# A GpSimd write and a wait for it ahead of each of 880 gathers in a graph layer

## The chip, the cores and the metric

The kernel runs on one core of a Trainium2 chip. The metric is the device time of one execution in microseconds (us). The core's engines, by the names of the profile, are PE (TensorE's matmuls; PEld is its weight loads), DVE (VectorE), ACT (ScalarE), POOL (GpSimd) and SP (SyncE, which here only issues transfers). Each has its own queue of instructions and works through it in order; they meet through semaphores.

## The reference

The input is 3125 nodes of 256 features, 53125 edges with a source, a destination and one of 16 types, and the weights of three blocks. The part that matters here is the typed message pass, done once along the edges and once against them:

```python
def _typed_pass(feat, W, bias, src_idx, dst_idx, etypes, norm_per_edge, n):
    proj = jnp.einsum('ni,rio->rno', feat, W)
    m = proj[etypes, src_idx] + bias
    m = m * norm_per_edge[:, None]
    return segment_sum(m, dst_idx, num_segments=n)
...
x = x + gnn(layernorm(x)) + mixer(layernorm(x))
x = x + moe_ffn(layernorm(x))
```

`norm_per_edge` is one over the degree of the node that receives. The mixer is a linear attention and an MLP over the same nodes; the last block routes each node to 2 of 8 experts.

## The kernel before, in words

The program is written out instruction by instruction, one queue per engine, with every wait stated. Three parts of it concern the change.

**Projection.** For each direction PE multiplies 25 tiles of 128 nodes with 16 weight matrices: `project` (line 674), 200 slots per direction, two matmuls of 512 columns in each. ACT copies every result out (`evacuate`, line 667) and SP stores it to a table in device memory, `table_fwd` or `table_bwd` (`store_banks`, line 685): one row of 256 floats for each node and type.

**Gather and sum.** The edges are sorted on the chip into 440 groups of 128 per direction (`TE`), each group with receivers in one tile of 128 nodes. For group `n`, POOL issues an indirect DMA that fetches 128 rows of 1 KB from the table into one of 16 buffers (`RING = 16`, `gather`, line 721). PE multiplies the buffer with a one-hot matrix (`sum_tile`, line 738), and DVE adds the result into the accumulator of its node tile (`add_sums`, line 764). The semaphore `s_sm` counts finished sums; gather `n` waits until sum `n - 16` is done, so that its buffer is free. That is the wait on line 724, which goes through the helper `Engine.wait` (line 74; it leaves out a wait for zero or less, so gathers 0 to 15 have none).

**Order of the work.** PE's order is fixed when the program is written. The sums of the forward groups stand between the backward projection's slots (`forward_upto`, line 781), 424 of them by the last slot; the other 16 and the 440 backward ones stand between the steps of the mixer: its rows and keys (`rows_upto`, `keys_upto`), attention (`attn_upto`) and MLP (`mlp_step`), whose last step comes with the last sum. POOL's queue in the meantime holds the gathers alone (lines 990 to 996). Ahead of the first gather it waits for the forward table to be stored, ahead of gather 440 for the backward table. After gather 879 POOL helps with additions (line 1001), and in the last block it issues 56 gathers of tokens (line 1009) and 56 indirect adds of rows to the output (line 1017, in `add_rows`), each of which waits first for its rows (`s_o7`, line 1013) and then for the indirect add before it (`s_sc`, line 1016, again through line 74).

ACT's `evacuate` has, at every even slot but the first few, two waits as well: first line 670 (that the store buffer is free), then line 671 (that the projection is done), and at every odd slot line 671 alone.

Of the kernel before, what the change touches and what calls it, by code (L numbers as in the profile page):

```python
# [101 lines left out]
def build(nc, a, out):  # L102
# [12 lines left out]
    with ctx:  # L115
        def sb(name, cols, dt=f32, rows=P):
            return ctx.enter_context(nc.sbuf_tensor(name, [rows, cols], dt))
# [5 lines left out]
        def sem(name, whole=False):  # L123

            nsem[0] += 1
            s_ = nc.alloc_semaphore(f"{name}_{nsem[0]}")
            if not whole:
                scope.append(s_)
            return s_

        def sems(name, n, whole=False):
            return [sem(f"{name}{i}", whole) for i in range(n)]
# [44 lines left out]
        kmax = sb("kmax", C)  # L177
        Pm = sb("Pm", 512)
        gmap_b = sb("gmap_bwd", TE, i32, 1)

        s_v, s_a = sem("dve", True), sem("act", True)
        V = Engine(None, nc.vector, s_v)
# [106 lines left out]
        RING = 16  # L289
# [424 lines left out]
        oh = [ar(R2 + RING * W + j * P, P) for j in range(RING)]  # L714
        acc = [ar(ACCF, NT * W), ar(R1, NT * W)]
        NARROW, SEG = (1, 6, 7), (2, 3, 6, 7)
        s_ga = sems("gather", RING)
        s_oh, s_sm, s_ac, s_ones, s_zf, s_zb = (sem(n) for n in
            ("onehots", "segment_mm", "accumulated", "ones_set", "zero_forward", "zero_backward"))

        def gather(e, n):

            d, b = n // TE, n % RING
            G.wait(s_sm, n - RING + 1)
            e.indirect_dma_start(msg[b][:, 0:C], None, table[d], bass.IndirectOffsetOnAxis(  # L725
                ap=idx[d][:, n % TE:n % TE + 1], axis=0)).then_inc(s_ga[b], 16)

# [251 lines left out]
        with nc.Block() as block:  # L979
            @block.gpsimd  # L980
            def _(e):
# [8 lines left out]
                for n in range(TE):  # L990
                    gather(e, n)
# [3 lines left out]
                for n in range(TE, 2 * TE):  # L995
                    gather(e, n)
# [1014 lines left out]
```

## Time and profile before

| | us |
|---|---|
| median of 3 runs | 2249.82 (2246.55 to 2253.24) |
| the profiled execution | 2245.63 |
| its span, first to last instruction | 2243.7 |
| PE busy | 2015.8 (90%) |
| POOL busy | 1027.6 (46%) |
| DVE busy | 1138.3 (51%) |
| ACT busy | 605.0 (27%) |
| DMA engines, mean share over the span, queue of the gathers (q0) | 23.1% |

The profile is of one execution. Busy time counts an engine's own instructions, not its sequencer's waits and branches. PE's granted clock is 0.960 of full speed over the span. In a timeline row stand the start, the duration, the engine, the line, what is written and read, and in brackets how long the engine had been idle and what ended that; "issue" stands for time in which it waited for nothing that the profile shows, "remote" for a releaser that the profile doesn't know.

### The profile page before, as it was taken

The page shows a single profiled execution, that of the slowest core. Times are in us where ns is not written, and L with a number is a line of the kernel's source. Part 1 is how long each engine was busy: PE and PEld are TensorE (multiplying, and loading weights), DVE is VectorE, ACT ScalarE, POOL GpSimd, SP SyncE. Part 2 cuts the span into 40 slices and gives each one's busy share as a digit, 9 for nine tenths or more (in the row PEclk, how much of TensorE's full clock was granted, in tenths as well). Part 3 has the DMA queues.
Part 4 walks back from the last instruction along what each step waited for, and adds up shares of the span by engine and source line. Part 5 has one row for each costly group of instructions (what it writes and reads, how often), then busy time and mean ns, then how long its engine had stood idle before and what let it go on. Part 6 is the DMA issues. An engine that isn't in the chain of part 4 may idle for free.

```text
span 2243.7 us, 26429 instructions
## 1 busy us (share of the span) xinstructions
PE 2015.8 (90%) x8235; PEld 1379.3 (61%) x8235; DVE 1138.3 (51%) x2452; ACT 605.0 (27%) x1262; POOL 1027.6 (46%) x1014
## 2 busy tenths in 40 slices
PE   7999999889999999898878788898989669999997
PEld 3456544355555555454545555677777668888897
DVE  4999950256666564433566656544455841111121
ACT  2333333211221221111422221222222552222242
POOL 0000000366666666666566666666665113333332
PEclk9999999999999999999899999999999579999999
DMA  7432335455555555556644444332334384444473
GB/s 276 158 136 95 134 155 229 159 158 177 179 178 179 178 168 182 178 181 165 184 144 138 146 138 122 90 90 87 87 90 80 128 288 112 125 116 120 128 194 67
DMA packets 136486, 333.20 MB, mean 149 GB/s; under 512 B 25344, under 2 KB 65952, under 8 KB 135072
## 3 DMA queue, kind: packets, MB, share of 16 engines
q1 hardware_dynamic: 80064, 199.64, 24.5%
q0 software_dynamic: 52992, 130.09, 23.1%
q10 hardware_dynamic: 3296, 1.80, 0.3%
q8 instruction: 71, 1.16, 0.2%
q14 instruction: 63, 0.52, 0.1%
HBM read 202.71 MB, written 128.71 MB: 148 GB/s over the span
## 4 chain that ended last, share of the span: by engine, by line
PE 80%; issue 6%; another core or an unknown queue 5%; DVE 4%; ACT 3%; DMA 2%; DVEq 0%; POOL 0%; SPq 0%; ACTq 0%; POOLq 0%
PE bank L679 29%; PE bank L748 15%; PE bank L1947 9%; PE bank L1958 8%; PE bank L1867 4%; PE bank L1876 4%; PE bank L586 3%; DVE arena L773 1%; PE bank L1777 1%; PE bank L1805 1%; DMA table_fwd<-arena 1%; PE bank L1765 1%; PE bank L1844 1%; PE bank L1916 1%
## 5 line engine op out<-in xcount | busy, mean ns | idle before, releaser
L679 PE MATMUL bank<-arena,work 128*128 128x512 f32 x1600 | 741.9, 600 | 14.2 <-ACT arena L672 9.0
L773 DVE TENSOR_TENSOR arena<-arena,bank 128x257 f32 x880 | 370.8, 421 | 529.7 <-PE bank L748 284.1
L748 PE MATMUL bank<-arena 128*128 128x257 f32 x1760 | 499.2, 396 | 71.1 <-DVE arena L773 37.6
L725 POOL DMA_INDIRECT arena<-table_bwd,arena x440 | 428.3, 974 | 237.4 <-issue 99.0
L725 POOL DMA_INDIRECT arena<-table_fwd,arena x440 | 437.2, 994 | 212.8 <-issue 99.8
L679 PEld LDWEIGHTS bank<-arena,work 128*128 128x128 f32 x1600 | 301.3, 192 | 296.5 <-issue 270.8
L672 ACT ACTIVATE arena<-bank 128x512 f32<-128x512 f32 x400 | 238.5, 598 | 777.4 <-PE bank L679 551.7
L748 PEld LDWEIGHTS bank<-arena 128*128 128x128 f32 x1760 | 327.7, 197 | 194.8 <-issue 153.7
L1017 POOL DMA_INDIRECT out<-xn,work x56 | 89.4, 1597 | 250.9 <-DVE xn L192 181.3
L1947 PE MATMUL bank<-xn,arena 128*128 128x256 f32 (+1 forms) x1120 | 203.0, 340 | 0.0
L734 DVE TENSOR_TENSOR arena<-cst,arena 128x512 f32<-128x512 f32 x220 | 151.2, 689 | 102.0 <-PE bank L679 102.0
L1958 PE MATMUL bank<-arena 128*128 x896 | 199.0, 379 | 0.0
L1691 ACT ACTIVATE arena<-bank,work 128x256 f32<-128x256 f32 (+1 forms) x280 | 120.6, 431 | 286.7 <-PE bank L1947 278.5
L1947 PEld LDWEIGHTS bank<-xn,arena 128*128 128x128 f32 x1120 | 178.9, 192 | 17.0
L1486 DVE TENSOR_TENSOR xn<-bank,work 128x256 f32<-128x256 f32 x56 | 23.8, 425 | 321.5 <-PE bank L1958 321.5
L1958 PEld LDWEIGHTS bank<-arena 128*128 128x128 f32 x896 | 169.2, 190 | 22.4
L984 POOL MEMSET arena<- 128x6425 f32 x1 | 5.5, 5453 | 313.5 <-DVE gmap_bwd L193 313.5
L1867 PE MATMUL bank<-arena 128*128 128x256 f32 (+1 forms) x416 | 111.2, 390 | 25.7 <-ACT arena L1642 14.8
L1876 PE MATMUL bank<-arena 128*128 128x256 f32 x400 | 106.4, 388 | 8.0 <-ACT arena L1642 6.2
L1867 PEld LDWEIGHTS bank<-arena 128*128 128x128 f32 x416 | 79.2, 198 | 45.7 <-ACT arena L1642 19.4
L586 PEld LDWEIGHTS bank<-arena,work 128*128 128x128 f16 x832 | 67.2, 97 | 51.1 <-issue 46.5
L508 DVE TENSOR_TENSOR arena<-arena 128x648 f16<-128x648 f16 (+1 forms) x156 | 92.4, 607 | 8.8 <-PE bank L586 7.1
(315 smaller groups left out, 1563.8 us busy)
## 6 DMA issues: line engine op xcount, KB each, us to landing
table_fwd<-arena SPq DMA_DIRECT2D x100, 512.0 KB
table_bwd<-arena SPq DMA_DIRECT2D x100, 512.0 KB
arena<-in_W SPq DMA_DIRECT2D x35, 1024.0 KB
arena<-in_W SPq DMA_DIRECT2D x2, 4096.0 KB, 14.3
arena<-table_fwd,arena POOLq DMA_INDIRECT x440
arena<-table_bwd,arena POOLq DMA_INDIRECT x440
work<-x_transposed SPq DMA_DIRECT2D x50, 128.0 KB
mix_rows<-arena SPq DMA_DIRECT2D x25, 256.0 KB
```

The lines of the kernel that those rows point to most:

```text
L586: last = pe.matmul(ps[bank][:, 0:2 * LT].rearrange("p (v l) -> p v l", v=2), ohv[:, c // QB, :, c % QB], abv[:, :, c // QB, :, c % QB], st ...
L672: act.activation(ar(STG0 + s % 8 * 512, 512), ps[4 + s % 2][:, :], ACT.Copy).then_inc(s_po, 1)
L679: last = pe.matmul(ps[4 + s % 2][:, :], xT[t % 2][:, k * P:(k + 1) * P], ar(W_off[d] + k * 4096 + c * 512, 512), start=(k == 0), stop=(k = ...
L725: e.indirect_dma_start(msg[b][:, 0:C], None, table[d], bass.IndirectOffsetOnAxis(ap=idx[d][:, n % TE:n % TE + 1], axis=0)).then_inc(s_ga[b ...
L734: vec.tensor_tensor(oh_all[:, b:b + 4, :], iota.unsqueeze(1).broadcast_to(four), loc[n // TE][:, c:c + 4].unsqueeze(2).broadcast_to(four), ...
L748: pe.matmul(ps[sum_bank(n)][:, 0:W], oh[b], msg[b], start=True, stop=True).then_inc(s_sm, 1)
L773: vec.tensor_tensor(to, to, ps[sum_bank(n)][:, 0:W], ALU.add).then_inc(s_ac, 1)
L1691: act.activation(hT7[u % 2][:, j * C:j * C + n], ps[1 + j % 4][:, 0:n], ACT.Gelu, bias=aux[u % AR][:, 4 + j:5 + j]).then_inc(s_c7, 1)
L1867: last = pe.matmul(ps[4 + j % 2][:, 0:n], ar(W1T_off + k * HID + j * P, P), z2T[:, k * C:k * C + n], start=(k == 0), stop=(k == 1))
L1876: pe.matmul(bank, hT[:, j * C + u * P:j * C + (u + 1) * P], ar(W2T_off + j * C, C), start=(j == 0), stop=False)
L1947: last = pe.matmul(ps[1 + j % 4][:, 0:n], w1b[u % 4][:, k * HID + j * P:k * HID + (j + 1) * P], xT7[u % 2][:, k * C:k * C + n], start=(k = ...
L1958: last = pe.matmul(ps[5 + t % 2][:, 0:C], h, arena[:, ds(x * 2048 + (WE2 + j * C), C)], start=(j == 0), stop=(j == 7))
```

## The change

`gather` first writes zeros to a new tile of one column, `pause`, with a memset on GpSimd that adds one to a new semaphore, `s_pause`. After the wait for a free buffer and ahead of the indirect DMA it waits until `s_pause` has reached `n + 1`, that is, until this memset is done. Nothing reads the tile.

```diff
         gmap_b = sb("gmap_bwd", TE, i32, 1)
+        pause = sb("pause", 1)
...
-        s_ga = sems("gather", RING)
+        s_ga, s_pause = sems("gather", RING), sem("pause")
...
         def gather(e, n):
 
             d, b = n // TE, n % RING
+            nc.gpsimd.memset(pause[:, :], 0.0).then_inc(s_pause, 1)
             G.wait(s_sm, n - RING + 1)
+            e.wait_ge(s_pause, n + 1)
             e.indirect_dma_start(msg[b][:, 0:C], None, table[d], bass.IndirectOffsetOnAxis(
                 ap=idx[d][:, n % TE:n % TE + 1], axis=0)).then_inc(s_ga[b], 16)
```

## Rows read from the trace of the kernel before

**Rows 1.** The page, the chain that ended last, by engine.
```profile
PE 80%; issue 6%; another core or an unknown queue 5%; DVE 4%; ACT 3%; DMA 2%; DVEq 0%; POOL 0%; SPq 0%; ACTq 0%; POOLq 0%
```

**Rows 2.** Groups of POOL: busy us, mean ns, idle before and what ended it.
```profile
L725 POOL DMA_INDIRECT arena<-table_fwd,arena x440 | 437.2, 994 | 212.8 <-issue 99.8 <-PE bank L748 65.2 <-remote 43.4
L725 POOL DMA_INDIRECT arena<-table_bwd,arena x440 | 428.3, 974 | 237.4 <-issue 99.0 <-PE bank L748 95.3 <-remote 34.9
```

**Rows 3.** The line of the gathers: durations in ns (least, median, most), who waited.
```profile
L725 POOL DMA_INDIRECT arena<-table_fwd,arena x440: 940/946/1496, 420.7 to 1065.4; - x147
L725 POOL DMA_INDIRECT arena<-table_bwd,arena x440: 940/946/1412, 1074.6 to 1731.1; - x147
...
who waited for it (us, times):
  PEld bank L748: 3.7, 1
  PE bank L748: 2.8, 1
```

**Rows 4.** Windows, instructions of line 748 alone: PE and PEld busy (count), clock, DMA.
```profile
420.00:800.00 380.00, 132.97 (x488) 86.79 (x488) 0.98 0.56 173
420.00:1066.00 646.00, 229.77 (x848) 153.65 (x848) 0.98 0.57 174
```

**Rows 5.** Windows, instructions of line 725 alone: POOL busy (count), clock, DMA.
```profile
420.00:800.00 380.00, 260.87 (x258) 0.98 0.56 173
420.00:1066.00 646.00, 436.90 (x440) 0.98 0.57 174
```

**Rows 6.** Windows, all: PE, PEld, DVE, ACT, POOL busy (count), clock, DMA.
```profile
420.00:1066.00 646.00, 588.52 (x2109) 342.64 (x2107) 341.61 (x758) 126.11 (x227) 436.90 (x440) 0.98 0.57 174
1075.00:1732.00 657.00, 553.76 (x2289) 418.72 (x2289) 374.37 (x913) 158.23 (x353) 427.90 (x440) 0.95 0.40 116
```

**Rows 7.** Timeline of POOL, the first gathers, and around the last forward one.
```profile
416.21 0.13 POOL L986 MEMSET arena<- 128x16 f32 x1 [96.78 <-PE bank L679]
420.70 1.14 POOL L725 DMA_INDIRECT arena<-table_fwd,arena  x1 [4.36 <-DMA table_fwd<-arena]
...
1060.40 0.94 POOL L725 DMA_INDIRECT arena<-table_fwd,arena  x1 [1.45 <-PE bank L748]
1061.65 0.95 POOL L725 DMA_INDIRECT arena<-table_fwd,arena  x1 [0.30 <-issue]
...
1074.61 0.94 POOL L725 DMA_INDIRECT arena<-table_bwd,arena  x1 [8.27 <-DMA table_bwd<-arena]
```

**Rows 8.** Timeline of PE: the first two sums, and the last two (two instructions each).
```profile
424.89 1.14 PE L748 MATMUL bank<-arena 128*128 128x257 f32 x4 [2.84 <-DMA arena<-table_fwd,arena]
...
1744.38 1.03 PE L748 MATMUL bank<-arena 128*128 128x257 f32 x4
```

**Rows 9.** Timeline of POOL, its memsets at the start, back to back.
```profile
0.25 0.10 POOL L2005 MEMSET const-float32-0.0<- 128x1 f32 x1 [0.25 <-issue]
0.28 0.10 POOL L2005 MEMSET const-float32-1.0<- 128x1 f32 x1
```

**Rows 10.** The chain that ended last, the kernel's end: start us, us, what.
```profile
2228.12 0.36 DVE xn L192
2228.49 0.39 issue
2228.88 3.62 DMA out<-xn,work
2232.49 0.02 issue
2232.52 0.02 POOLq L74
2232.54 0.77 issue
2233.31 1.55 POOL out L1017
```

**Rows 11.** Timeline of SP, the transfer that waits for the backward table as well.
```profile
1073.84 0.81 SPq L1083 DMA_DIRECT2D arena<-in_mW1T  x2
```

**Rows 12.** The chain that ended last, in the backward projection.
```profile
922.67 0.02 ACTq L671
922.68 0.04 issue
922.73 0.60 ACT arena L672
```

**Rows 13.** Waits of PE from 420 to 1745 us: total us, times, longest.
```profile
PE bank L748 <- DVE arena L773: 37.6, 24, 6.8
```

## The prediction

> **What bounds the kernel now.** I began with the chain of waits that ended last. PE holds 80% of it and POOL none to speak of [rows 1]: matmuls set the time, and a POOL instruction is free as long as the gathers keep ahead of the sums.
>
> How far ahead are they? The groups of POOL show 880 gathers with a mean of (437.2 + 428.3) / 880 = 0.98 us [rows 2]. By the row of their line, 440 start from 420.7 to 1065.4, so one per 644.7 / 439 = 1.469 us, and 440 from 1074.6 to 1731.1, one per 656.5 / 439 = 1.495 us [rows 3]. Is that POOL's own pace or one imposed on it? Two gathers that wait for nothing stand 1.25 us apart, 0.95 us of work and a gap of 0.30 us; now and then one waits, as at 1060.40, for a sum of PE [rows 7]. The windows say the same: by 800 us there are 258 gathers [rows 5] and 488 / 2 = 244 sums, by 1066 us 440 gathers and 848 / 2 = 424 sums [rows 4]. So POOL runs 14 to 16 groups ahead, which is the whole ring, and PE waited for a gather once or twice in 1312 us (3.7 and 2.8 us) [rows 3]. PE, busy for 588.5 of 646 and 553.8 of 657 us [rows 6], paces the gathers through `s_sm`.
>
> POOL's spare time is then small: 1.469 less its own pace. That pace is the mean duration, 0.98, and 0.30, so 1.28 us; the spare is 0.19 us a gather forward and 0.21 backward. What the change adds up to 0.19 us costs nothing (PE hides it). Beyond that POOL becomes the bound, 880 times over. The question is the length of the stop.
>
> **The stop, step by step.** (1) The memset stands in POOL's queue behind gather n-1, so it is done only after that one. From the gather's end to the memset's start no row shows this pair; the ends are 0.03 us (four memsets back to back start 0.03 us apart, [rows 9]) and 0.30 us (gather to gather, [rows 7]). I take 0.10: a memset is nearer to the first, and even alone a gather begins late (below). (2) The memset of one column: 0.10 us [rows 9], 0.13 us for 16 columns on the same partitions [rows 7]. I take 0.11. (3) From the semaphore to the gather's start. Here lies most of the cost, and it depends on which of the two waits rides with the gather.
>
> [...] In the chain at the kernel's end the indirect add of L1017 has two waits, first `s_o7`, then `s_sc` by the helper on L74, and a row of POOL's queue bears the name of the second: POOLq L74, 0.02 us [rows 10]. ACT's evacuation has first L670, then L671, and again the second stands alone, ACTq L671 [rows 12]. So the first wait in the order of the program rides. In the changed gather `s_sm` comes first, and the wait for `s_pause` stands alone ahead of the indirect DMA from gather 16 on.
>
> What does that cost? At the end the scatter lands at 2232.49, the lone wait ends at 2232.54, and the next indirect DMA starts 0.77 us later; from landing to start 0.82 us. When the last wait to be met is the one that rides, VectorE's result, which ends at 2228.48, releases the same instruction in 0.40 us at most [rows 10]. Gather 440 has lone waits too: the backward table's landing starts an SP transfer at 1073.84 [rows 11] and the gather at 1074.61 [rows 7], 0.77 us. [...] I take 0.76 us from the memset's end to the gather's start, by the gather's own row; the ends are 0.40 us (the preparation hidden after all) and 0.82 us.
>
> Period of a gather: 0.98 + 0.10 + 0.11 + 0.76 = 1.95 us, against 1.469 and 1.495 now. Ends: 0.98 + 0.03 + 0.10 + 0.40 = 1.51, and 0.98 + 0.30 + 0.13 + 0.82 = 2.23 us.
>
> [...]
>
> **The sum.** The first gather starts at 420.70 [rows 7]. Gathers 1 to 15 have only the new wait, which rides. The 0.40 us above hold VectorE's own way out as well, so I take 0.28: 0.98 + 0.10 + 0.11 + 0.28 = 1.47 us each, 22.1 us together, to 442.8. The other 864 take 1.95 us: 1684.8 us, to 2127.6. The last sum follows its gather's start by what the first ones show with an empty ring: 424.89 less 420.70 is 4.2, less for later ones; I take 3.2, to 2130.8. Today the last sum starts at about 1744.9 (the second of the pair from 1744.38 [rows 8]). The difference is 386 us. The pause of 8.27 us ahead of gather 440 [rows 7] goes: sum 424, with the last backward projections, then runs some 3 us behind gather 424, 15 gathers or 29 us ahead of gather 439, and the stores end in that time. The uniform 864 periods have this in them already.
>
> What is behind POOL's wait? Its queue holds only gathers until 879. PE's sums wait for them, and behind these, since PE's order is fixed, all the projections and the mixer. Does PE keep up? It needs (588.5 + 553.8) / 880 = 1.30 us a group [rows 6], DVE 0.81 us, and the ring still evens out stretches of PE without sums. So POOL's period sets the stretch. Outside it nothing moves: after the last sum the program is the same, 499 us. The 880 memsets themselves (97 us) are within the period.
>
> Against the profiled execution: 2245.6 + 386 = 2631.6 us. That execution lies 4 us under the median of the three runs, so a median might be 2636; I stay between them at 2632.
>
> **The rivals.** (a) No change. If the wait for `s_pause` rode with the gather (or the preparation overlapped the wait), the period would be 1.47 us, today's, and the ring's head start would even out the rest: 2246 to 2252 us. It decides at 0.19 us of added time a gather. For it: the added instruction alone is 0.11 us, and its write is trivial. Against it: both pairs of waits in the trace leave the second alone. [...] (c) Longer: the memset starts 0.30 us after the gather and the lone wait costs 0.82, period 2.23: 442.8 + 1926.7 + 3.2 - 1744.9 = +628 us, 2873 us. For it: the gap of 0.30 us is the only one that follows a gather in the trace. (d) Faster: the stop lets VectorE, which shares work on the same memory, run without POOL beside it. PE waited 37.6 us for VectorE's additions at the sums [rows 13], so 2208 us at best, and only with all of the stop hidden.
>
> **How the numbers follow.** The forecast, a period of 1.85 to 2.14 us: 0.80, and by the same sum 2545 to 2796 us. (a) 0.08, (b) 0.05, (c) 0.05, (d) 0.02. The range 2530 to 2800 holds the forecast and the upper end of (b), a little over 8 in 10. The runs of before spread by 0.3%, about what can be told from no change, 7 us. Faster by more: (d), 0.02. Within: (a), 0.08. Slower: the forecast, (b) and (c), 0.90.
>
> **What would show it.** In the changed trace: a POOLq row of the new wait, or POOL's gathers without idle time ended by `s_sm`; starts of gathers 1.95 us apart, 1.47 us for the first 15; a memset 0.1 us behind each gather's end, then some 0.76 us idle before the next; PE waiting for gathers at L748 hundreds of times where it was once; sums level with gathers in the windows, not 14 behind; last gather near 2127 us; PE's share of the chain far under 80%; no 8 us gap ahead of gather 440; and 499 us after the last sum as now. It would be wrong if the starts stay 1.47 us apart (the wait is hidden), if the memset starts or lasts much later or longer than 0.2 us in all, or if PE falls behind on its own at the lower granted clock that idle time may bring (0.95 to 0.98 now).

## The result, and the profile after

The changed kernel takes 2546.13 us (median of 4 runs, 2543.91 to 2552.76) against 2249.09 us for the kernel before on the same chip: a ratio of 1.1326, 95% interval 1.1306 to 1.1347. The profiled execution took 2552.76 us, its span is 2550.9 us. The forecast was 2632 us.

First the chain that ended last, by engine (the page of the changed kernel; before in [rows 1]):

```profile
PE 52%; DMA 31%; issue 8%; POOL 7%; ACT 2%; DVE 0%; POOLq 0%; DVEq 0%
```

PE has fallen from 80% to 52%, and what has come in is the landing of gathers (DMA) and POOL. The line of the gathers and who waited for it (durations in ns; before in [rows 3]):

```profile
L728 POOL DMA_INDIRECT arena<-table_fwd,arena x440: 944/944/1464, 419.1 to 1234.5; - x147
L728 POOL DMA_INDIRECT arena<-table_bwd,arena x440: 944/944/1422, 1236.3 to 2048.7; - x147
...
who waited for it (us, times):
  PEld bank L751: 573.2, 579
  PE bank L751: 326.9, 431
```

From start to start the gathers now need (1234.5 - 419.1) / 439 = 1.857 us forward and (2048.7 - 1236.3) / 439 = 1.851 us backward, against 1.469 and 1.495. PE's matmuls waited for them 431 times, where they had waited once.

The timeline of POOL shows the stop itself, first at gathers 14 to 16, then where the tables change (before in [rows 7]):

```profile
438.54 0.95 POOL L728 DMA_INDIRECT arena<-table_fwd,arena  x1 [0.27 <-POOL pause L725]
439.49 0.11 POOL L725 MEMSET pause<- 128x1 f32 x1
439.87 0.94 POOL L728 DMA_INDIRECT arena<-table_fwd,arena  x1 [0.27 <-POOL pause L725]
440.81 0.11 POOL L725 MEMSET pause<- 128x1 f32 x1
441.68 0.94 POOL L728 DMA_INDIRECT arena<-table_fwd,arena  x1 [0.75 <-issue]
...
1234.45 0.94 POOL L728 DMA_INDIRECT arena<-table_fwd,arena  x1 [0.75 <-PE bank L751]
1235.40 0.11 POOL L725 MEMSET pause<- 128x1 f32 x1
1236.26 0.94 POOL L728 DMA_INDIRECT arena<-table_bwd,arena  x1 [0.75 <-issue]
```

The reader is to see three things. Each memset starts with the end of the gather ahead of it (439.49, 440.81) and takes 0.11 us. Gathers 1 to 15, which have the new wait alone, start 0.27 us after the memset; from gather 16 on, with both waits, 0.75 us after it. And the pause of 8.27 us ahead of the first backward gather is gone. That the 0.75 us are behind a lone wait shows in the chain (start us, us, what):

```profile
1005.56 0.12 POOL pause L725
1005.68 0.02 issue
1005.71 0.02 POOLq L727
1005.72 0.70 issue
1006.42 0.94 POOL arena L728
```

POOLq L727 is the wait for `s_pause`, and 0.70 us of "issue" follow it, as 0.77 us followed the lone wait of [rows 10].

How far the gathers are ahead: in the windows from 420 to 1066 us, line 751 alone (PE, PEld), then line 728 alone (POOL); before in [rows 4, 5]:

```profile
420.00:1066.00 646.00, 217.13 (x694) 115.03 (x694) 0.97 0.46 141
```
```profile
420.00:1066.00 646.00, 344.21 (x349) 0.97 0.46 141
```

694 / 2 = 347 sums stand against 349 gathers: the ring is empty where it had been full. What is left after the last sum (from 2052 us; PE, PEld, DVE, ACT, POOL):

```profile
2052.00:2551.00 499.00, 450.88 (x2388) 405.70 (x2388) 137.13 (x350) 173.38 (x408) 156.26 (x128) 0.92 0.52 144
```

The last sum starts at 2052.28 us, 307.5 us later than before (1744.82), and the span has grown by 307.2 us. The whole loss lies in the stretch of the gathers.

### The profile page after: what moved, and what is told of

It reads as the page before. It is cut to its first block, busy times and chain, and to the rows that moved or that the text cites. A ratio compares the mean times of both kernels' runs of the same rounds, so it can differ in the third digit from the quotient of the medians.

```text
span 2550.9 us, 28172 instructions
## 1 busy us (share of the span) xinstructions
PE 2140.6 (84%) x8235; PEld 1358.7 (53%) x8235; DVE 1149.7 (45%) x2452; ACT 606.8 (24%) x1262; POOL 1117.9 (44%) x1894
## 4 chain that ended last, share of the span: by engine, by line
PE 52%; DMA 31%; issue 8%; POOL 7%; ACT 2%; DVE 0%; POOLq 0%; DVEq 0%
PE bank L680 18%; DMA arena<-table_bwd,arena 15%; DMA arena<-table_fwd,arena 14%; PE bank L751 11%; PE bank L1950 8%; PE bank L1961 7%; POOL arena L728 6%; PE bank L587 2%; PE bank L1879 1%; POOL pause L725 1%; DMA table_fwd<-arena 1%; PE bank L1919 1%; ACT arena L1677 1%; PE bank L1780 1%; PE bank L1939 1%
## 5 line engine op out<-in xcount | busy, mean ns | idle before, releaser
L751 PE MATMUL bank<-arena 128*128 128x257 f32 x1760 | 590.0, 428 | 339.9 <-DMA arena<-table_bwd,arena 171.8
L751 PEld LDWEIGHTS bank<-arena 128*128 128x128 f32 x1760 | 291.2, 196 | 626.5 <-DMA arena<-table_bwd,arena 309.9
L728 POOL DMA_INDIRECT arena<-table_bwd,arena x440 | 423.0, 961 | 341.1 <-PE bank L751 218.0
L1961 PEld LDWEIGHTS bank<-arena 128*128 128x128 f32 x896 | 169.2, 190 | 22.4
L1645 ACT ACTIVATE arena<-bank,small 128x256 f32<-128x256 f32 (+1 forms) x104 | 48.5, 466 | 237.7 <-PE bank L1870 213.1
L725 POOL MEMSET pause<- 128x1 f32 x880 | 99.3, 113 | 4.6 <-DMA table_fwd<-arena 3.8
```

What stands on the lines that cost most here:

```text
L725: nc.gpsimd.memset(pause[:, :], 0.0).then_inc(s_pause, 1)
L751: pe.matmul(ps[sum_bank(n)][:, 0:W], oh[b], msg[b], start=True, stop=True).then_inc(s_sm, 1)
L1961: last = pe.matmul(ps[5 + t % 2][:, 0:C], h, arena[:, ds(x * 2048 + (WE2 + j * C), C)], start=(j == 0), stop=(j == 7))
```

## The experiments

The diffs are against the changed kernel.

The preparation theory says: the 0.70 us between the row of the lone wait and its indirect DMA (the chain above) are exposed because the wait is met only after the gather ahead has ended; met earlier, they lie within that gather. No row of a trace shows what POOL does in these 0.70 us, or that anything is prepared; "preparation" is a name for the time that the runs below make appear and disappear. "Rides" is such a name too: it is said of the wait that has no row in POOL's queue, where the other, lone one has a row of 0.02 us (POOLq). The theory's rivals: the stop costs this however it is waited for, a further wait on the sequencer costs it whenever it is met, or the memset itself costs.

**A caution on the base.** The kernel before took 2249 us in the first session, 2079 in the second and 2231 in the third. What is called the second session here are two, on two different chips: 2078.61 us beside the first four experiments and 2079.94 beside the next four. The third ran on yet another chip. No program ran twice on one chip in different sessions, as far as the chips are known, so no run shows whether the chip makes the difference. Each experiment is compared with the kernel before in its own session.

**The waits in the other order.**

```diff
             nc.gpsimd.memset(pause[:, :], 0.0).then_inc(s_pause, 1)
-            G.wait(s_sm, n - RING + 1)
             e.wait_ge(s_pause, n + 1)
+            G.wait(s_sm, n - RING + 1)
```

> The changed kernel with its two waits in the other order: first for the memset, then for the free buffer, so that the wait for the memset rides with the gather and the one for the buffer stands alone. Preparation theory (the cost is the preparation of the indirect DMA, which the lone wait for the memset keeps from running beside the gather ahead): the first 15 gathers of the changed trace have a riding wait and start 0.27 us after the memset, so starts are 0.97 + 0.11 + 0.27 = 1.35 us apart where nothing else holds them, under the 1.469 that PE leaves; 2249 us, within 0.3%. Stop theory (a wait for a memset between two gathers costs 0.75 us however it is made): starts 1.81 us apart, 2546 us as changed.

Measured: 2155.68 us against 2078.61, ratio 1.0372 (1.0348 to 1.0397). Its timeline of POOL:

```profile
1002.01 0.11 POOL L725 MEMSET pause<- 128x1 f32 x1
1002.39 0.94 POOL L728 DMA_INDIRECT arena<-table_fwd,arena  x1 [0.27 <-POOL pause L725]
1003.33 0.11 POOL L725 MEMSET pause<- 128x1 f32 x1
1003.72 0.94 POOL L728 DMA_INDIRECT arena<-table_fwd,arena  x1 [0.27 <-PE bank L751]
```

Starts are 1.33 us apart (1.400 in the mean), near the 1.35 of the preparation theory, and 0.48 us of each stop are gone by the order of two lines. The stop theory falls. But the time did not return to that of the kernel before, as I had expected from the 1.469 us of the first session. In the second session PE leaves POOL less time, which the next runs show.

**The memset without a wait.**

```diff
-        pause = sb("pause", 1)
+        pause = sb("pause", 2 * TE, mybir.dt.uint8)
...
-            nc.gpsimd.memset(pause[:, :], 0.0).then_inc(s_pause, 1)
+            nc.gpsimd.memset(pause[:, n:n + 1], 0).then_inc(s_pause, 1)
             G.wait(s_sm, n - RING + 1)
-            e.wait_ge(s_pause, n + 1)
```

> The memset alone, of a column of its own for each gather (one byte wide, so that they fit), with nothing that waits for it. Preparation theory: 0.11 us more a gather at most, 1.28 + 0.11 = 1.39 us, hidden; 2249 us. A rival: the memset as an instruction on the same engine costs by itself, for example by a longer gap ahead of the gather that follows it (over 0.41 us from the gather's end to the next start, against 0.30 before): 2249 us plus 864 times what the period has over 1.48 us.

Measured: 2080.73 us, ratio 1.0002 (0.9992 to 1.0012).

```profile
1000.92 0.94 POOL L727 DMA_INDIRECT arena<-table_bwd,arena  x1 [0.19 <-PE bank L750]
1001.87 0.12 POOL L725 MEMSET pause<- 128x1 uint8 x1
1002.17 1.12 POOL L727 DMA_INDIRECT arena<-table_bwd,arena  x1 [0.19 <-issue]
```

Starts are 1.25 us apart, as without a memset: it lies inside the 0.30 us that POOL has between two gathers anyway. Even the 0.11 us that I had allowed are not paid. The memset as such costs nothing.

**The wait one gather ahead.**

```diff
-        pause = sb("pause", 1)
+        pause = sb("pause", 2)
...
-            nc.gpsimd.memset(pause[:, :], 0.0).then_inc(s_pause, 1)
+            nc.gpsimd.memset(pause[:, n % 2:n % 2 + 1], 0.0).then_inc(s_pause, 1)
             G.wait(s_sm, n - RING + 1)
-            e.wait_ge(s_pause, n + 1)
+            G.wait(s_pause, n)
```

> The memset as changed, but the gather waits for the memset ahead of the gather before it (s_pause has reached n, not n + 1; two columns in turn). The wait stands alone as in the changed kernel, but is met while gather n - 1 has only just begun. Preparation theory: the preparation runs beside gather n - 1 again; starts 1.25 to 1.42 us apart, 2249 us. Lone-wait theory (a further wait on the sequencer costs 0.7 us each time, whenever it is met): 1.81 us apart, 2546 us. In between, if the preparation outlasts what is left of gather n - 1: 0.7 us against 0.94 us, so it should not.

Measured: 2086.47 us, ratio 1.0038 (1.0027 to 1.0049).

```profile
1001.30 0.12 POOL L725 MEMSET pause<- 128x1 f32 x1
1001.61 0.95 POOL L728 DMA_INDIRECT arena<-table_bwd,arena  x1 [0.19 <-POOL pause L725]
1002.55 0.11 POOL L725 MEMSET pause<- 128x1 f32 x1
1002.86 0.95 POOL L728 DMA_INDIRECT arena<-table_bwd,arena  x1 [0.19 <-POOL pause L725]
```

The same memset and a lone wait in the same place, and the period is 1.25 us again instead of 1.81. Only the moment at which the wait is met has moved.

Its 8 us over the kernel before are clear of the interval, and the traces show where they lie. Eight gathers (113, 211, 309, 407, 505, 603, 701 and 799, that is every 98th) start 1.8 to 2.0 us after the end of the gather ahead, though their buffers had been free for 4 us or more. Beyond the usual 0.30 us these eight stops take 13 us; the second session's trace of the kernel before has none of them. Gather 113 (idle time behind its memset):

```profile
567.46 0.95 POOL L728 DMA_INDIRECT arena<-table_fwd,arena  x1 [1.69 <-issue]
```

Other gathers wait less for their buffers in turn, so that all gaps from gather 16 on are together 10 us longer than in the kernel before (288.4 against 278.4). What makes every 98th gather late is open: the stops stand at these gathers in the changed kernel too, in those with the waits swapped and in the one with a stop at every second gather. The two kernels of the same session without a memset or without a wait for it have none of this size there.

**A second wait that is always met.**

```diff
-            nc.gpsimd.memset(pause[:, :], 0.0).then_inc(s_pause, 1)
             G.wait(s_sm, n - RING + 1)
-            e.wait_ge(s_pause, n + 1)
+            e.wait_ge(s_pj, SLOTS)
```

> No memset. The gather of the kernel before, with a second wait behind the one for the free buffer, for the count of projections that was reached before the first gather. It stands alone on the sequencer and is always met. Preparation theory: nothing is exposed, starts 1.25 us apart where no sum is waited for, 2249 us. Lone-wait theory: 0.7 us more a gather, period 0.98 + 0.75 = 1.73 us at least, about 2475 us.

Measured: 2080.32 us, ratio 1.0001 (0.9991 to 1.0012). The line of the new wait, and POOL's timeline:

```profile
L726 POOLq EVENT_SEMAPHORE  x865: 17/17/43, 419.6 to 1559.8; - x173
```
```profile
1000.90 0.97 POOL L727 DMA_INDIRECT arena<-table_bwd,arena  x1 [0.30 <-issue]
1002.17 0.95 POOL L727 DMA_INDIRECT arena<-table_bwd,arena  x1 [0.30 <-issue]
```

865 lone waits are in the program and nothing is lost: the lone-wait theory falls. In these runs a lone wait costs only when it is met late: the gap between two gathers is 0.30 us here, as in the kernel before, and 0.11 + 0.75 us in the changed kernel.

No run was made for one rival: that POOL takes 0.7 us to go on from any lone wait that is met late, whatever stands behind it. The trace of the kernel before speaks against it. POOL's first addition (line 1001) has two waits, and the second, for ACT's result (`s_bw`, line 1000), stands alone and is met last:

```profile
1747.92 0.51 ACT L1657 ACTIVATE arena<-arena,small 128x256 f32<-128x256 f32 x1 [0.71 <-DVEq L1326]
1748.58 0.87 POOL L1001 TENSOR_TENSOR X<-X,arena 128x256 f32<-128x256 f32 x1 [16.53 <-ACT arena L1657]
```

ACT ends at 1748.43, the row of the lone wait starts at 1748.46, and the addition starts 0.10 us after that row, where an indirect DMA starts 0.70 to 0.77 us after it. ACT's copy likewise starts 0.04 us behind its lone wait [rows 12]. So the 0.70 to 0.77 us stand in these rows only ahead of an indirect DMA; for POOL this rests on one place in one trace.

**The kernel before and the changed one once more.** Nothing is edited.

> The kernel before, unchanged, for a trace beside the experiments: in their session it took 2079 us where it had taken 2249 us, and they show the same instructions outside the stretch of the gathers. Pace theory (in that session PE is quicker through the sums, so that POOL's own pace of 1.25 us and its longer gathers, 1.32 us in the mean, set the stretch): about 2079 us, starts 1.25 us apart and 1.32 in the mean, sums 3 to 18 us behind the gathers. If the session is like the first, 2249 us and 1.47 us.

> The changed kernel, unchanged. Preparation theory: POOL's period is its own and the same on any chip, 1.81 us and 1.86 in the mean, so the time is near 2546 us also where the kernel before takes 2079 us: the change then costs 864 x (1.862 - 1.318) = 470 us. Proportional rival (the session is quicker in all): 1.13 x 2079 = 2354 us.

Measured: 2079.38 us, ratio 1.0007 (0.9994 to 1.0019), and 2549.01 us, ratio 1.2254 (1.2227 to 1.2281). The line of the gathers in the kernel before, second session:

```profile
L725 POOL DMA_INDIRECT arena<-table_fwd,arena x440: 942/949/1458, 417.6 to 992.7; - x147
L725 POOL DMA_INDIRECT arena<-table_bwd,arena x440: 942/949/1465, 996.0 to 1569.0; - x147
...
who waited for it (us, times):
  PEld bank L748: 33.4, 41
  PE bank L748: 14.4, 26
```

Here 1.310 us (575.1 / 439 forward; 1.305 backward) separate two gathers, POOL's own 1.25 with its longer ones, and PE waits for some of them. In the second session POOL was already next to being the bound. The changed kernel has the period of the first session (1.863 against 1.862 us from gather 16 on) and its time: 2549 against 2546 us. So the time after the change is set by POOL's period, and what the change costs, 297 or 469 us, by what POOL had to spare. With 1.310 as the base the swapped kernel's +77 us are explained: 864 x (1.400 - 1.310) = 78.

**A stop at every second and at every fourth gather.**

```diff
-            nc.gpsimd.memset(pause[:, :], 0.0).then_inc(s_pause, 1)
+            if n % 2 == 0:
+                nc.gpsimd.memset(pause[:, :], 0.0).then_inc(s_pause, 1)
             G.wait(s_sm, n - RING + 1)
-            e.wait_ge(s_pause, n + 1)
+            if n % 2 == 0:
+                e.wait_ge(s_pause, n // 2 + 1)
```

The other has 4 in place of 2.

> The memset and the wait for it, with the free-buffer wait first as in the changed kernel, at every second gather alone. Preparation theory: starts alternately 1.25 and 1.81 us apart, 1.53 us and with the longer gathers 1.58 in the mean; where the kernel before takes 2079 us (period 1.318) that is 864 x 0.262 = +226 us, 2305 us; where it takes 2249 us, a replay of its sums gives +55 us, 2304 us. If a stop disturbed more than its own gather, more than that.

> The memset and the lone wait for it at every fourth gather. Preparation theory, from the rows of the every-second kernel: three starts 1.25 us apart and one 1.81, 1.39 us, and 0.05 for the longer gathers, 1.445 in the mean. Where the kernel before takes 2079 us: 864 x (1.445 - 1.310) = +117 us less what the lead of the gathers takes up in the forward half (up to 18 us), 2180 to 2196 us. Where it takes 2249 us (1.47 to 1.495 left by the sums): nothing, 2249 us. The cost of the change thus depends on how much spare time POOL has, and not on the stop alone.

Measured: every second, 2305.16 us against 2079.94 in the second session, ratio 1.1082 (1.1057 to 1.1107), +225 us where +226 was expected. Every fourth, 2236.62 us against 2230.90 in the third session, ratio 1.0030 (1.0020 to 1.0040). The timelines of POOL, every second and then a stop of every fourth:

```profile
1001.64 0.94 POOL L730 DMA_INDIRECT arena<-table_fwd,arena  x1 [0.30 <-issue]
1002.58 0.11 POOL L726 MEMSET pause<- 128x1 f32 x1
1003.45 0.95 POOL L730 DMA_INDIRECT arena<-table_fwd,arena  x1 [0.75 <-POOL pause L726]
```
```profile
1003.75 0.12 POOL L726 MEMSET pause<- 128x1 f32 x1
1004.62 0.94 POOL L730 DMA_INDIRECT arena<-table_fwd,arena  x1 [0.75 <-POOL pause L726]
```

The stop is the same 0.11 + 0.75 us in both. At 1.58 us a gather it shows one for one; 220 of these stops cost 6 us where POOL had time to spare, clear of the interval though none was expected, against 220 x 0.56 = 123 us if each were paid. In these runs the cost is no price per stop: it depends on what POOL has to spare.

**A longer memset.** The order is that of the swapped kernel, and the tile is wider:

```diff
-        pause = sb("pause", 1)
+        pause = sb("pause", 256)
```

> The waits in the other order (the wait for the memset rides), and the memset 256 columns wide. The long memset of the kernel before took 5.45 us for 6425 columns, 0.85 ns a column, so this one takes 0.11 + 0.22 = 0.33 us. Additive theory: the period of the swapped kernel, 1.400 us in the mean, plus 0.22 = 1.62 us; 2156 + 864 x 0.22 = 2343 us. If a part of the memset is hidden behind the 0.27 us start of the gather, less.

Measured: 2327.77 us, ratio 1.1190 (1.1163 to 1.1216), 172 us over the swapped kernel of the same order; 187 were expected. (The two ran on the two chips of the second session, where the kernel before took the same within 1.4 us.)

```profile
1001.61 0.33 POOL L725 MEMSET pause<- 128x256 f32 x1
1002.21 0.95 POOL L728 DMA_INDIRECT arena<-table_fwd,arena  x1 [0.27 <-POOL pause L725]
```

The memset took the 0.33 us worked out, and the gather still starts 0.27 us after it, so nothing of it is hidden there: 864 x 0.212 = 183 us. The mean period grew by 0.198 us (1.400 to 1.598), 171 us; the other 12 us are other waits of the swapped kernel, 7 us shorter here, and gathers that last 5 us less in all. Once POOL is the bound, the longer memset is paid nearly in full.

**The kernel before in a third session.** Nothing is edited.

> The kernel before, unchanged, in a third session: 2079 us and no idle time of PE put down to nothing, as in the second; or 2249 us with PE idle for some 62 us that no record explains between 420 and 1720 us, as in the first. Either tells whether 2249 or 2079 us is what most sessions show; neither changes what the stop costs POOL.

Measured: 2230.95 us, ratio 0.9996 (0.9984 to 1.0007). PE's waits there and in the second session, 420 to 1720 us (total us, times, longest), third first:

```profile
PE bank L748 <- DVE arena L773: 30.6, 17, 11.0
PE bank L748 <- issue: 26.4, 25, 2.7
```
```profile
PE bank L748 <- DMA arena<-table_bwd,arena: 11.7, 25, 1.3
PE bank L1765 <- DMA work<-x_transposed: 11.0, 2, 8.6
```

In the first and the third session PE stands idle for "issue", that is, for nothing that the profile shows, in pieces of up to 6 us; in the second it never does in this stretch. This is only a part of the difference. From the first gather to the last sum the kernel before takes 1325 us in the first session (420 to 1745) and 1160 in the second (417 to 1577). PE is idle for 164 of the 1325 us and 49 of the 1160: some 60 us of the first are "issue", and waits for DVE's additions are 37.6 us [rows 13] against 3.3. PE is also busy for 1161 us against 1111, at a granted clock of 0.96 against 0.99. What sets all this off is open: no run changed it. It is not the rest of the program (outside the stretch of the gathers the traces run alike, within 4 us at the start and 2 at the end). Since every fourth ran only in the third session, its small loss shows what spare time hides there, and is not to be set beside the second session's every second.

## Why the prediction was right, and where its size was off

**The bound and its spare time.** Right for the session it was read from: PE paced the gathers, and POOL had about 0.2 us to spare. I took this pace for the kernel's own. In the second session PE was quicker and there were 0.03 us to spare or none. The predicted time was safe from that, since it stands on POOL's period and not on PE's; the rival of no change was not: had the new wait ridden, as in the swapped kernel, there would have been 77 us to pay in the second session, at a mean period of 1.400 us, while the first session's pace of 1.469 might have hidden it (that was not run).

**Which wait rides.** Right, and shown both ways. In the changed trace gather 15 starts 0.27 us after its memset and gather 16 0.75 us; the wait for `s_pause` has 864 rows in POOL's queue (L727) and the one for the buffer none, since L74 has only 55, those of the indirect adds. In the swapped kernel L74 has 919 rows, 864 more, the wait for `s_pause` none, and the gathers start 0.27 us after the memset. That the first wait goes to the engine with its instruction no row shows; the rows show only that it has none of its own.

**The lone wait, 0.76 us.** Measured 0.75, in the chain 0.02 + 0.02 + 0.70. The 0.77 us read from [rows 10, 11] held, and in the two runs with a lone wait that is met early this time is not in the gaps: 0.30 us from gather to gather in the one, 0.19 us from memset to gather in the other. That it is a preparation by the sequencer, which goes on beside the gather ahead, was my guess, and no run shows it. The rows show where the time stands: behind a lone wait that is met late, 0.70 to 0.77 us ahead of an indirect DMA, against 0.10 us ahead of POOL's addition.

**From the gather's end to the memset, 0.10 us.** This is the term that was mis-sized: it measured 0.00 (438.54 + 0.95 = 439.49, 439.87 + 0.94 = 440.81, and likewise in every pair of rows above). 864 x 0.10 = 86 us, which is most of the miss. That 2632 less 2546 is 86 as well is chance. The terms, 864 times each: this one 86 us too many, the lone wait 9, the mean gather 6; the memset 3 too few, and 22 for longer waits that the sum did not have (below). That is 864 x (1.95 - 1.862) = 76 us. With 3 us from the start and the first 15 gathers it makes the 79 us between the forecast growth of 386 us and the measured 307.5; the other 7 us are that the profiled execution lies that much over the median. The row of memsets back to back [rows 9] had been the nearest one, and I moved away from it toward the 0.30 us between gathers. These 0.30 us turn out to be the start of the gather that follows, not the end of the one before: a memset fits into them whole.

**The rest of the sum.** The memset 0.11 as taken (0.113). The mean gather 0.973 for 0.98. The first gather at 419.06 for 420.70, the first 15 periods 1.39 us in the mean (12 of them 1.33 to 1.36) for 1.47. The last sum 3.6 us behind its gather for 3.2. The measured period, 0.973 + 0.00 + 0.113 + 0.75 = 1.836, and 1.862 in the mean: 15 gathers waited longer, 21 us together or 0.025 a gather. They did not wait for PE, whose sums had freed their buffers over 24 us before. Eight are every 98th gather, 113 to 799, and start 3.26 us after the end of the gather ahead; seven (66, 194, 322, 492, 620, 748, 876) lie 128 apart within each direction and start 1.17 us after it. The trace on the other chip has the same gathers and gaps. Gather 113 (the usual idle time behind the memset is 0.75 us):

```profile
623.86 0.95 POOL L728 DMA_INDIRECT arena<-table_fwd,arena  x1 [3.15 <-issue]
```

The sum had no term for this, and its cause is open.

**How much was luck.** The measured period of 1.862 us lies just inside the forecast of 1.85 to 2.14. Without those 15 waits it would have been 1.837, under the forecast's lower end, and the time about 2525 us, below the range of 2530 to 2800. So an error that made the stop too long was covered in part by waits that nobody had foreseen.

**What goes.** The 8.27 us pause ahead of gather 440 went, and the 499 us after the last sum stayed. PE kept up, as these windows of the changed trace show (all engines: PE, PEld, DVE, ACT, POOL busy, count; clock, DMA):

```profile
420.00:1234.00 814.00, 651.02 (x2150) 343.95 (x2150) 354.28 (x777) 137.69 (x247) 481.16 (x878) 0.97 0.47 142
1236.00:2052.00 816.00, 632.16 (x2327) 409.61 (x2325) 381.61 (x912) 157.57 (x351) 472.58 (x879) 0.94 0.32 91
```

It was busy for 651 of 814 and 632 of 816 us where it had been busy for 588.5 of 646 and 553.8 of 657 [rows 6]: it idles more and still arrives with the gathers. The granted clock fell only from 0.98 and 0.95 to 0.97 and 0.94.

## What to carry to other kernels

In these traces the first of a gather's two waits has no row of its own and the second stands alone in POOL's queue (864 rows). Where the second was met by the memset, the indirect DMA started 0.75 us after it; where the first was, 0.27 us after it. Here it paid to put the wait that is met last first (2155.68 us, 1.0372 of the kernel before) or to wait one gather ahead (2086.47 us, 1.0038), against 1.2254 for the changed kernel in the second session. Before adding anything to an engine that only feeds another, compare its own period (starts that wait for nothing) with the pace that is imposed on it: here it was nearly free up to the difference (6 us for 220 stops of 0.56 us), beyond it it counted nearly in full once per gather (172 us where 864 x 0.212 is 183), and the difference itself varied between sessions (about 0.2 us in the first, 0.03 or none in the second).

## What the runs showed of the hardware that I had not expected

A memset of one column between two gathers costs no time that shows: with it the gap is 0.00 + 0.12 + 0.19 us, without it 0.30. The row of a lone wait (POOLq) stands 0.03 us behind the memset's end in the changed kernel (1005.71), and also where its condition was met a gather earlier (1001.45 in the run that waits one gather ahead). So such a row does not tell whether its wait was met late; the time from the memset's end to the gather does (0.19 or 0.75 us). In the kernels in which every gather, or every second, waits for a memset every 98th gather starts late, by 2.4 us in the changed one. And the same program took 2249, 2079 and 2231 us in different sessions, by PE's idle and busy time in the stretch of the gathers, while the changed one took 2546 and 2549.
